# A fused attention and feed-forward layer on one core: where TensorE's loop over units is closed

## The reference

```python
q = (x @ Wq.T + bq).reshape(B, S, H, D)          # B=8, S=1024, H=16, D=32
k = (x @ Wk.T + bk).reshape(B, S, H, D)
v = (x @ Wv.T + bv).reshape(B, S, H, D)
q, k = rope(q), rope(k)
qk  = einsum('bshd,bstd->bsht', q, k) / sqrt(D)  # heads against heads at one position
att = softmax(qk)
out = einsum('bsht,bstd->bshd', att, v)
out = swapaxes(out, 1, 2).reshape(B, S, E)
x = layernorm(x + out @ Wo.T + bo)
g = (x @ gate_w.T) * gate_s ; u = (x @ up_w.T) * up_s
x = layernorm(x + ((silu(g) * u) @ down_w.T) * down_s)
```

## Time and profile before

| | us |
|---|---|
| timed runs | 1739.11, 1741.29, 1742.19 (median 1741.29) |
| profiled execution, its own time | 1744.73 |
| span of the profiled execution | 1742.9 |
| TensorE matmul busy | 1698.9 (97%) |
| VectorE busy | 1376.6 (79%) |
| ScalarE busy | 943.2 (54%) |
| GpSimdE busy | 813.5 (47%) |

### The profile page before, as it was taken

How to read it: one execution, slowest core, us unless ns; L and a number is a source line. 1 busy time by engine, 2 the same in 40 slices (tenths; PEclk the granted TensorE clock), 3 DMA queues, 4 the chain that set the end, 5 groups by cost and what they waited for, 6 DMA issues and landing times.

```text
span 1742.9 us, 40756 instructions
## 1 busy us (share of the span) xinstructions
PE 1698.9 (97%) x15138; PEld 1392.2 (80%) x15138; DVE 1376.6 (79%) x1972; ACT 943.2 (54%) x1461; POOL 813.5 (47%) x700
## 2 busy tenths in 40 slices
PE   8899999999999999999999999999999999999997
PEld 6777888888888888887788888888888888888885
DVE  7988999999999999998867667676676766767656
ACT  5554555655555565556645455554555646556453
POOL 6887888888888888888200201102011020110112
PEclk9999999999999999999999999999999999999998
DMA  7486777677778977875863553534536344354351
GB/s 215 99 178 161 160 171 176 169 154 178 176 161 192 204 187 156 178 178 121 255 221 105 176 169 105 183 116 152 171 102 198 121 156 154 111 183 148 106 184 49
DMA packets 444598, 278.06 MB, mean 160 GB/s; under 512 B 258816, under 2 KB 383104, under 8 KB 444544
## 3 DMA queue, kind: packets, MB, share of 16 engines
q1 hardware_dynamic: 444544, 277.37, 59.4%
HBM read 183.97 MB, written 93.32 MB: 159 GB/s over the span
## 4 chain that ended last, share of the span: by engine, by line
PE 91%; DVE 4%; issue 3%; POOL 1%; ACT 1%; DMA 0%; POOLq 0%; DVEq 0%; ACTq 0%; SPq 0%
PE ps_x L666 13%; PE ps_x L670 12%; PE ps_x L667 12%; PE ps_s L830 9%; PE ps_s L835 9%; PE ps_x L830 7%; PE ps_x L835 7%; PE ps_x L841 4%; PE ps_x L845 4%; PE ps_s L743 3%; PE ps_a L700 2%; PE ps_a L841 2%; PE ps_a L845 2%; PE ps_s L841 2%; PE ps_s L845 2%
## 5 line engine op out<-in xcount | busy, mean ns | idle before, releaser
L666 PE MATMUL ps_x<-wqkv_hi,xc_hi 128*128 128x512 f32 x768 | 305.3, 397 | 19.1 <-issue 8.9
L670 PE MATMUL ps_x<-wqkv_hi,xc_lo 128*128 128x512 f32 x768 | 301.4, 392 | 0.0
L1407 POOL TENSOR_TENSOR z<-z,xr 128x512 f32<-128x512 f32 x60 | 77.2, 1311 | 480.3 <-DVE z L1752 480.3
L667 PE MATMUL ps_x<-wqkv_lo,xc_hi 128*128 128x512 f32 x768 | 301.1, 392 | 0.0
L830 PE MATMUL ps_s<-x_hi,slot 128*128 128x512 f32 x672 | 264.1, 393 | 0.6 <-DVE hid L1683 0.3
L835 PE MATMUL ps_s<-x_lo,slot 128*128 128x512 f32 x672 | 261.8, 390 | 0.0
L1000 ACT ACTIVATE kX<-kT 32x512 f32<-32x512 f32 x256 | 160.8, 628 | 163.9 <-DVE kT L1486 161.7
L1274 POOL TENSOR_TENSOR qk_cos<-qk_in,rot 128x512 f32<-128x512 f32 x128 | 203.0, 1586 | 70.7 <-DVE qk_in L1463 51.0
L830 PE MATMUL ps_x<-x_hi,slot 128*128 128x512 f32 x560 | 218.9, 391 | 0.8 <-ACT hid L1120 0.4
L835 PE MATMUL ps_x<-x_lo,slot 128*128 128x512 f32 x560 | 217.9, 389 | 0.0
L1280 POOL TENSOR_TENSOR qk_cos<-qk_cos,qk_sin 128x512 f32<-128x512 f32 x128 | 204.0, 1594 | 10.0
(11 more groups left out here) (119 smaller groups left out, 3703.5 us busy)
## 6 DMA issues: line engine op xcount, KB each, us to landing
slot<-gu_hi SPq DMA_DIRECT2D x88, 896.0 KB, 5.0
xc<-x_cols SPq DMA_DIRECT2D x32, 512.0 KB, 5.6
v_rows<-v_in SPq DMA_DIRECT2D x32, 512.0 KB, 4.3
v<-v_rows SPq DMA_DIRECT2D x32, 512.0 KB, 5.1
res<-x_rows SPq DMA_DIRECT2D x64, 256.0 KB, 3.6
x_rows<-x_out SPq DMA_DIRECT2D x32, 512.0 KB, 2.8
x_cols<-x_turn SPq DMA_DIRECT2D x128, 128.0 KB
wide<-x_cols SPq DMA_DIRECT2D x64, 256.0 KB, 5.1
```

The costliest lines, as they stand in the source:

```text
L666: pe.matmul(out, hi[:, k], w_hi[w][:, k], start=(k == 0), stop=False)
L667: pe.matmul(out, hi[:, k], w_lo[w][:, k], start=False, stop=False)
L670: last = pe.matmul(out, lo[:, k], w_hi[w][:, k], start=False, stop=(k == KE - 1))
L1407: pool.tensor_tensor(z[:, h, r], z[:, h, r], rows_of_x1(n, h)[:, r], ALU.add).then_inc(z_added[h], 1)
```

## The change

Step s is cut in two: `begin_step(s)` is `project_qk(s - 1, 0)`, and `finish_step(s)` is all the rest. Ahead of the loop stand step 4 and the beginning of step 5. The loop's body is the end of step i and the beginning of step i + 1, and behind the loop stands the end of step 32. The matmuls and their order are the same; the loop is closed behind the first tile's products of keys and queries, not behind the scores.

```diff
-            def step(s):
+            def begin_step(s):
+                project_qk(s - 1, 0)
+
+            def finish_step(s):
                 if (m := unit_of(s, 1, UNITS)) is not None:
-                    project_qk(m, 0)
                     project_qk(m, 1)
                     project_v(m)
...
-            unit_steps(pe, step, LAGS, UNITS, 1)
+            for s in range(OPENING, LAGS):
+                begin_step(s)
+                finish_step(s)
+
+            begin_step(LAGS)
+            with pe.Fori(LAGS, UNITS) as i:
+                finish_step(i)
+                begin_step(i + 1)
+            finish_step(UNITS)
```

## The result

The changed kernel takes 1728.8 us (median of 5 runs, 1726.07 to 1731.34) against 1741.29 us (5 runs, 1738.76 to 1742.19): ratio 0.9928, 95% interval 0.9915 to 0.9941, 12.5 us less. The forecast was 1733.0 us, 8.3 us less, with a range down to 1729.8 us. The time fell out of that range on the fast side. The changed kernel was timed three times more, each time beside the kernel before on the same chip: 1730.76 (ratio 0.9937), 1729.69 (0.9934) and 1730.68 us (0.9938), against 1741.50, 1740.95 and 1740.79 us, so 10.1 to 11.3 us less. The gain is about 11 us, and the first measurement lies above that. Of these three medians two lie inside the predicted range and the third 0.1 us outside it, so part of the first miss is chance.

The account below looks back on a forecast made before the run. TensorE was taken to bound the kernel, standing idle at 26 taken loop closings; 0.32 us saved at each gives 8.3 us, so 1741.29 - 8.3 = 1733.0 us, with a range of 1729.8 to 1738.0 us.

Parts of the forecast that it names:

- What bounds the kernel: Attention loop: TensorE is busy 97% of the span, so a microsecond it stands still is a microsecond of the kernel.
- a taken closing costs 0.36 to 0.40 us: Scores to second product: 2.31 us with the branch taken, 1.95 at the loop's exit, 1.91 in the opening without closing.
- The leftover behind the scores: Register work and waits that stay behind the scores cost 0.08 us per turn, leaving a gain of 0.32 us.
- the exit's row: Where the loop is left, two control instructions between burst and product cost 0.04 us; taken as the leftover's lower bound.
- even split: Upper bound of the leftover: four control instructions at 0.10 us each, two staying, 0.20 us; gain 5.2 us.
- Rival 1: Behind the scores: register work is the cost, not the jump; gain 5.2 us or down to 3; chance 0.14.
- The new place costs nothing: Closing behind the 24 products: the sequencer is ahead there and hides the jump; without cover 0.35 us per turn.
- Rival 3: Behind the bursts: nothing changes, whatever follows the burst that runs the sequencer dry pays; 1741.3 us; chance 0.05.
- Rival 4: Behind the first tile's products: the jump's time goes along, 3.9 us more, 1745.2 us; chance 0.04.
- VectorE keeps its margin of 0.18 us: Heads' input: VectorE's low half ends 0.18 us before TensorE starts the heads; both count from the keys, so no shrinking.
- Rival 2: Heads' input: VectorE takes over, so TensorE gains only 0.18 us per turn, 4.7 us, 1736.6 us; chance 0.05.
- the late fetches of rows 11: Instruction fetches late in or behind bursts, 2.6 to 2.7 us each: put at no change, 2.7 us either way.

Follow-up runs that it names:

- regs2: Changed kernel with two more register additions, each with a long-fulfilled wait, behind the scores in every turn: 1736.06 us, ratio 0.9964.
- regs6: Changed kernel with six more register additions, each with a long-fulfilled wait, behind the scores in every turn: 1747.03 us, ratio 1.003.
- close_k: Changed kernel with the loop closed 12 products earlier, behind the first tile's keys alone: 1730.89 us, ratio 0.9942.
- close_av: Changed kernel with the loop closed between the values' burst and the scores' burst, one turn less: 1746.02 us, ratio 1.0021.
- after_early: Changed kernel with VectorE's low half of the heads' input ahead of the last of four sines, 0.6 us sooner: 1730.82 us, ratio 0.9941.
- dve_late: Changed kernel with a 160-column fill on VectorE ahead of the low half of the heads' input in each turn: 1734.82 us, ratio 0.9954.
- close_v_swap: Changed kernel closed behind all 72 products, heads' product waiting for its bank first, for VectorE and ScalarE last: 1732.11 us, ratio 0.9943.

## Why the prediction was right or wrong, step by step

- **What bounds the kernel; a taken closing costs 0.36 to 0.40 us.** Right. 25 waits for issue went, and the turn fell from 25.38 to 25.03 us where 25.06 was forecast.
- **The leftover behind the scores, taken as 0.08 us.** Too large: 1.94 us against 1.91 leave 0.03 us. The gain per turn is 0.36 to 0.37 us, 9.4 to 9.6 us in 26, in place of 8.3. The choice between the exit's row (0.04 us) and an even split should have gone to the exit's row. Rival 1, that register work is the cost, is half true: regs2 and regs6 show 0.095 us for each further addition with its wait, close to the even split's 0.10 us. What the prediction did not see is that the first few are nearly free; that the sequencer's lead covers them is the reading that fits.
- **The new place costs nothing.** Right, 0.23 us between the 24th and the 25th product; 12 products cover it too (close_k), and one burst does not (close_av). Rival 3, that whatever follows the burst pays the idle time, did not happen: 0.03 us is left there. Rival 4, slower, had its mechanism right and its place wrong: it would have decided behind a burst.
- **VectorE keeps its margin of 0.18 us.** The cost was right and the margin wrong. It was measured to the matmul. The weight load in front of it starts 0.07 us behind VectorE's end in both kernels, and its delay is hidden only by the lead of loads over matmuls. It costs 0.03 to 0.04 us per turn (after_early), and in both kernels alike: from the last product ahead of the heads' to their last it takes 5.47 us in each, and 5.44 in after_early. So it cancels out, but dve_late shows that nothing is left: 0.11 us later on VectorE is 0.13 us on the turn. Rival 2 did not happen because VectorE's chain starts at the keys, and these came 0.36 us sooner, as argued.
- **Where the prediction failed: "the late fetches of rows 11 should stay; I put them at no change".** The gain came out 4.2 us above the forecast in the first measurement and about 2.7 us by the later ones. The leftover explains 1.1 to 1.3 us of that. This step is the largest of the rest: behind the loop the gap fell from 1.5 to 2.6 us to 0.6 us, worth 1.0 to 2.4 us. "Every instruction outside the body keeps its place within one or two" spoke of their order; where each stands in memory changes more, as the loop's first part is written out once more ahead of it and the body ends elsewhere. Moving the kernel before by 48 instructions gave the same better end in two profiles, and moving the changed kernel by 44 a worse one, so this part belongs to placement and not to the closing.
- **The clock behind the late fetches at the loop's entry, not thought of at all.** From burst 3 to 5 two late fetches stand in or right behind the scores, near 106 and 136 us, in every profile. Behind each the granted clock can fall. The page of the profile does not show it: its slices are 43.6 us long, and a digit 9 stands for anything from 0.90 up. A gap alone does not bring it either: in regs6 the gaps are 2.36 and 2.46 us, and the granted clock is 1.00 in both windows of the table below (in that run it had fallen to 0.91 from 60 to 100 us). Granted clock (fourth number) from 130 to 150 us in the second profiles, first of the kernel before, then of the changed one:

```profile
130.00:150.00 20.00, 17.21 (x307) 0.83 0.79 185
```

```profile
130.00:150.00 20.00, 18.08 (x317) 0.91 0.84 186
```

and TensorE's timeline of the kernel before in that profile:

```profile
136.53 1.81 PE L743 MATMUL ps_s<-kX,qT 64*32 64x64 f32 x106 [2.51 <-issue]
138.63 0.79 PE L666 MATMUL ps_x<-wqkv_hi,xc_hi 128*128 128x512 f32 x1 [0.28 <-issue]
139.22 0.63 PE L667 MATMUL ps_x<-wqkv_lo,xc_hi 128*128 128x512 f32 x1
139.64 0.63 PE L670 MATMUL ps_x<-wqkv_hi,xc_lo 128*128 128x512 f32 x1
```

Between 139 and 140 us the granted clock is 0.50, which is 1.2 GHz, and a product starts 0.42 us behind the one before it and not 0.23. With the loss taken as the length of the window times what is missing of the clock, and the gaps of the fetches and of the jump taken off, the stretch comes out alike in four profiles, so gaps and clock account for its differences within a microsecond (us; the clock of 100 to 115 us and of 130 to 150 us):

```
profile             burst 3 to 5   gaps          clock         loss   rest
before, second          60.14      2.48 + 2.79   0.89, 0.83    5.1    49.8
changed, first          54.02      0.93 + 2.44   1.00, 1.00    0      50.7
changed, second         57.41      2.07 + 1.92   0.89, 0.91    3.5    50.0
regs2                   57.64      2.07 + 2.42   1.00, 0.83    3.4    49.8
```

The first profile of the changed kernel is the shortest of the four because its clock did not fall in this stretch at all and its first gap is short (0.93 us). Whether a kernel gets 0.83 or 0.91 behind the second fetch is not settled: the kernel before had 0.83 in both its profiles and the changed one 0.91 in its second, third and fourth, but regs2 and close_v_swap, closed as the changed kernel or later, had 0.83. That the jump's gap behind the fetch keeps the clock down longer is therefore a guess that these runs do not bear out.
- **What the Trainium skill made of it.** Over the loop (150 to 800 us) the changed kernel shows, on the instruction queues,

```profile
q14 instruction: 7, 0.06, 0.0%
q8 instruction: 1, 0.02, 0.0%
```

one packet in 25 turns on queue 8, so the body is again not fetched at each turn, and the Trainium skill's rule of the forced fetch (Runtime: NRT & Kernel Launch, Instruction fetch mechanics) again does not show. The Trainium skill's 108 ns for a compare-and-branch (Advanced Engine Details and Errata, Control Flow Timing) gave 2.8 us as an estimate; measured were 9.4 to 9.6 us, 0.36 to 0.37 us for each taken closing behind the bursts, and nothing behind big products.

The profiles add up as follows. The second one of the kernel before is 13.9 us longer than the mean of the changed kernel's last three: 1.1 us ahead of burst 0, -0.3 from burst 0 to 3, 2.6 from 3 to 5 (which holds the 26th closing), 9.5 from 5 to 30, and 1.1 from burst 31 to the end. The medians give about 11 us. The 1.1 us ahead of burst 0 are scatter, and that execution of the kernel before, 1743.73 us, is 2.0 us above the kernel's median in the same measurement (1741.74 us). How much of the 2.6 us at the entry and of the end a median execution shows stays open.

## What to carry to other kernels

Close a hardware loop behind a stretch of long instructions, not behind or between bursts of short ones: here the closing cost 0.36 us behind the bursts, 0.46 between them, and nothing behind 12 or 24 big products, nor behind 72 once VectorE was early. Look at which instruction carries a late wait: register work that waits for a late engine runs only behind it, and so is paid in full even where the jump is free (put the wait that comes last on the product itself). And when code is written out again ahead of a loop, count late instruction fetches and what the clock does behind them as a term of 1 to 3 us of unknown sign, and not as nothing.

## What the runs showed of the hardware that was not expected

- A register addition with a fulfilled wait costs 0.095 us on TensorE's sequencer once the lead is used up, by two points (two: 0.19 us, six: 0.57 us).
- A burst of 128 short matmuls, 1.4 us long, is enough to use the lead up: the closing behind one burst (0.46 us) cost no less than behind two (0.40 us).
- The scores of the loop's first turn had a gap of a late instruction fetch in or behind them, 1.9 to 2.9 us and once 4.0, in every kernel that was profiled, whatever the place of the loop's closing; entering the loop one step later gave two (2.28 and 2.38 us) in place of one.
- A late fetch of 2.4 us can cost more than itself: where the granted clock was 0.91 or 0.83 over the 20 us from 130 to 150 us, 1.8 to 3.4 us went there besides the gap.
